# A mixture-of-experts layer on one core: expert rows are added to the residual by the transfers that fetch them

## The reference

```python
h = tok(x)
h = h + attn(layernorm(h))
# ffn, on xf = layernorm(h)
probs = softmax(xf @ router_w)
topw, topi = top_k(probs, 2)
combine = zeros.at[row, topi].add(topw)
ye = einsum('nef,efd->ned', silu(einsum('nd,edf->nef', xf, w1)), w2)
routed = einsum('ne,ned->nd', combine, ye)
shared = silu(gate) * up @ shared_down          # gate, up = xf @ shared_gate_up
shared = sigmoid(xf @ shared_gate_w) * shared
out = h + routed + shared
```

## Time and profile before

| | us |
|---|---|
| median of three runs | 1132.4 |
| lowest and highest | 1131.16, 1133.53 |
| the profiled execution | 1139.81 |
| its span, first to last instruction | 1138.0 |

### The profile page before, as it was taken

The page is one execution under the profiler, slowest core; times in us unless marked ns, Lnnn a source line. Parts: engine busy times, 40 slices in busy tenths (PEclk is TensorE's granted clock), DMA queues, the critical chain, the costliest instruction groups (busy, mean ns, idle before and its releaser), DMA issues.

```text
span 1138.0 us, 24005 instructions
## 1 busy us (share of the span) xinstructions
PE 1062.1 (93%) x8058; PEld 891.3 (78%) x8059; DVE 768.7 (68%) x1975; ACT 671.1 (59%) x2062; POOL 537.2 (47%) x575
## 2 busy tenths in 40 slices
PE   7979999999999999999999999999979798899985
PEld 6857788878877887877788788788858687898874
DVE  3757766785776678577667857766765954566666
ACT  4647765774775677477567747766774333454431
POOL 0025434554556455464545546454361746544542
PEclk9989999999999999999999999999999988999997
DMA  8110000000001000000100000010025423343494
GB/s 259 56 43 2 1 1 19 2 11 30 20 2 38 20 1 13 27 20 2 38 20 1 20 20 20 1 39 20 2 98 194 134 70 108 112 134 121 131 330 141
DMA packets 46624, 66.07 MB, mean 58 GB/s; under 512 B 7992, under 2 KB 39608, under 8 KB 45496
## 3 DMA queue, kind: packets, MB, share of 16 engines
q1 hardware_dynamic: 39720, 46.73, 13.1%
q0 software_dynamic: 6528, 17.97, 4.3%
q10 hardware_dynamic: 272, 0.00, 0.0%
HBM read 36.22 MB, written 28.46 MB: 57 GB/s over the span
## 4 chain that ended last, share of the span: by engine, by line
PE 72%; DVE 8%; issue 6%; POOL 5%; ACT 2%; another core or an unknown queue 1%; DMA 0%; DVEq 0%; SPq 0%; ACTq 0%; POOLq 0%
PE pT_ps L730 10%; PE o_ps L743 9%; PE proj_ps L68 9%; PE proj_ps L70 9%; PE proj_ps L69 9%; PE s_ps L716 8%; PE v_ps L68 2%; POOL prob L1676 2%; PE v_ps L69 2%; PE v_ps L70 2%; PE s_ps L68 2%; POOL prob L1678 2%; PE s_ps L70 2%; PE pT_ps L977 2%; PE s_ps L69 2%
## 5 line engine op out<-in xcount | busy, mean ns | idle before, releaser
L1039 ACT ACTIVATE prob<-s_ps,nmax 128x255 f32<-128x255 f32 x512 | 239.1, 478 | 227.7 <-DVE nmax L1251 227.6
L1676 POOL TENSOR_SCALAR prob<-prob,rinv 128x255 f32<-128x255 f32 x128 | 139.6, 1090 | 373.8 <-DVE rinv L1269 369.4
L1251 DVE TENSOR_REDUCE nmax<-s_ps 128x2 f32<-128x510 f32 x256 | 166.0, 681 | 37.9 <-PE s_ps L716 36.4
L730 PEld LDWEIGHTS pT_ps<-ident,prob 128*128 128x128 f32 x1024 | 109.8, 141 | 60.6 <-issue 49.7
L730 PE MATMUL pT_ps<-ident,prob 128*128 128x128 f32 x1024 | 146.2, 281 | 6.5 <-POOL prob L1678 3.4
L743 PE MATMUL o_ps<-probT,v 128*64 128x256 f32 x1024 | 139.6, 394 | 1.2 <-DVE oT_lo L1282 1.2
L1276 DVE COPY probT<-pT_ps 128x512 f32<-128x512 f32 x128 | 88.4, 691 | 77.0 <-PE pT_ps L730 77.0
L716 PE MATMUL s_ps<-qk_space 64*128 64x256 f32 x1536 | 125.2, 295 | 5.1 <-ACT prob L1039 4.4
L1678 POOL TENSOR_SCALAR prob<-prob,rinv 128x255 f32<-128x255 f32 x128 | 119.1, 931 | 0.0
L716 PEld LDWEIGHTS s_ps<-qk_space 64*128 64x128 f32 x1536 | 98.9, 185 | 21.8 <-issue 8.5
L1771 POOL DMA_INDIRECT expert_out_rows<-yg,y_at x72 | 69.4, 964 | 81.1 <-DVE yg L1581 45.4
(11 more groups left out here) (267 smaller groups left out, 2778.2 us busy)
## 6 DMA issues: line engine op xcount, KB each, us to landing
xg<-expert_in_rows SPq DMA_DIRECT2D x72, 130.0 KB
back<-expert_out_rows SPq DMA_DIRECT2D x8, 1024.0 KB, 9.4
xin<-in_x_dram SPq DMA_DIRECT2D x8, 512.0 KB, 4.4
z_rows<-z SPq DMA_DIRECT2D x8, 512.0 KB, 3.2
z<-z_rows SPq DMA_DIRECT2D x8, 512.0 KB
expert_in_rows<-bo_row SPq DMA_DIRECT2D x16, 128.0 KB
raw_up<-in_L_ffn_w_dram SPq DMA_DIRECT2D x8, 256.0 KB, 5.0
raw_down<-in_L_ffn_w_dram SPq DMA_DIRECT2D x8, 256.0 KB, 6.3
```

The lines of the kernel that those rows point to most:

```text
L730: m = pe.transpose(pT_ps[h][:, o:o + P], prob[u_par(i)][:, h, qt, kt * P:(kt + 1) * P], ident[:])
L1039: m = act.activation(prob[u_par(i)][:, h, qt, 1:N], s_ps[h][:, qt * N + 1:(qt + 1) * N], ACT.Exp, bias=nmax[u_par(i)][:, n:n + 1], accum_o ...
L1251: dve.tensor_reduce(nmax[u_par(i)][:, 2 * h:2 * h + 2], s_ps[h][:].rearrange("p (q k) -> p q k", q=2)[:, :, 1:N], AX_X, ALU.max, negate=Tr ...
L1676: pool.tensor_scalar(prob[k][:, 0, 1, 1:N], prob[k][:, 0, 1, 1:N], rinv[k][:, 1:2], None, ALU.mult).then_inc(s_nA1, 1)
```

## The change

The two results of a token no longer stand side by side: choice 0 of token r goes to row r of `y_rows`, choice 1 to row 4096 + r. The tiles `back`, the loads into them, and all additions of expert rows on DVE and POOL are gone. In their place POOL issues, for each group and choice, one transfer from `y_rows` in HBM to the group's rows of `resid` in SBUF with `accum_op=ADD`: 16 transfers of 512 KB. For a group the second choice's transfer waits until the first one's has landed. For groups 0 to 3 the first one waits for the gated addition, which was done before the loop. For groups 4 to 7 the order is turned round: the gated addition (`add_shared`) waits until both transfers have landed. A store waits for both. The issue order on POOL is 4, 5 (first), then 4, 5 (second) and 0, 1 (first), then 0, 1 (second), then 2, 3, 6, 7 (first) and 2, 3, 6, 7 (second), with `hidden_split_lo` of groups 4 and 5 in between and that of 6 and 7 behind them all.

```diff
             def store_group(g):
-                sp.wait_ge(s_all, g + 1)
+                sp.wait_ge(s_back[g], 16 * TOP)
                 sp.wait_ge(s_added, 2 * g + 2)
...
             load_z3(SHARED_EARLY + 2)
-            for k in range(UNROLL):
-                sp.wait_ge(s_yst[k], 16 * TURNS)
-            for g in range(2):
-                load_back(g)
             load_z3(SHARED_EARLY + 3)
-            for g in range(2, 5):
-                load_back(g)
             for g in range(GROUPS):
                 store_group(g)
-                if g + 5 < GROUPS:
-                    load_back(g + 5)
...
             def add_shared(g):
                 dve.wait_ge(s_gate, 2 * g + 2)
-                if g >= EXPERTS_FIRST:
-                    dve.wait_ge(s_all, g + 1)
-                else:
-                    dve.wait_ge(s_woe, 2 * g + 2 + FREE_W)
+                if g >= SHARED_EARLY:
+                    dve.wait_ge(s_back[g], 16 * TOP)
+                dve.wait_ge(s_woe, 2 * g + 2 + FREE_W)
...
-            pool.iota(dest_u[:], pattern=[[TOP, GT]], base=0, channel_multiplier=TOP * GT).then_inc(s_iotas, 1)
+            pool.iota(dest_u[:], pattern=[[1, GT]], base=0, channel_multiplier=GT).then_inc(s_iotas, 1)
...
-            pool.tensor_scalar(dest[:], dest_u[:], float(-TOP * GR), None, ALU.add)
+            pool.tensor_scalar(dest[:], dest_u[:], float(-GR), None, ALU.add)
...
-                        pool.tensor_scalar(z2_twice[:, n, :, D], dest[:], float(n), None, ALU.add)
+                        pool.tensor_scalar(z2_twice[:, n, :, D], dest[:], float(n * ROWS), None, ALU.add)
...
+            def add_experts(g, k):
+                if k:
+                    pool.wait_ge(s_back[g], 16)
+                else:
+                    pool.wait_ge(s_woe, 2 * g + 2 + FREE_W)
+                    if g < SHARED_EARLY:
+                        pool.wait_ge(s_added, 2 * g + 2)
+                rows = y_rows[ROWS * k + GR * g:ROWS * k + GR * (g + 1), :].rearrange("(p t) d -> p (t d)", t=GT)
+                pool.dma_start(resid[:, GT * g:GT * g + GT, :].rearrange("p t d -> p (t d)"), rows,
+                               accum_op=ALU.add).then_inc(s_back[g], 16)
+
+            for k in range(UNROLL):
+                pool.wait_ge(s_yst[k], 16 * TURNS)
+            for g in (4, 5):
+                add_experts(g, 0)
             hidden_split_lo(4)
-            pair_rows(0)
+            for g in (4, 5):
+                add_experts(g, 1)
+            for g in (0, 1):
+                add_experts(g, 0)
             hidden_split_lo(5)
-            pair_rows(2)
+            for g in (0, 1):
+                add_experts(g, 1)
+            for g in (2, 3, 6, 7):
+                add_experts(g, 0)
+            for g in (2, 3, 6, 7):
+                add_experts(g, 1)
             hidden_split_lo(6)
-            pair_rows(4)
             hidden_split_lo(7)
```

More of the change, by code:

```diff
@@ L469, in main_phase @@
         raw_up, raw_down = (over(n, first, 0, [DC, E, F]) for n, first in (("raw_up", at["oT_lo"]), ("raw_down", wo_at)))
-        back = [over(f"back{g}", (at["oT_hi"], at["oT_lo"], at["qk_space"], wo_at)[g // 2], g % 2 * GT * TOP * D,
-                     [GT, TOP, D]) for g in range(GROUPS)]
         xgT_hi, xgT_lo = ([over(f"{n}{k}", at["probT1"], (2 * j + k) * DC * P, [DC * P], F32R) for k in range(2)]
@@ L524, in main_phase @@
         s_back = [sem(f"back{g}_in") for g in range(GROUPS)]
-        s_pair, s_first, s_gate = sem("expert_rows_paired"), sem("first_added"), sem("gates_ready")
-        s_all, s_out = sem("rows_complete"), sem("out_stored")
+        s_gate = sem("gates_ready")
+        s_out = sem("out_stored")
         s_pgo = sem("pool_wait_met")
-        PAIRED_BY_POOL = (0, 2, 4)
-        EXPERTS_FIRST = 6
         def uses(r, k):
@@ L1599, in _ @@
             y_copy(TURNS - 1, UNROLL - 1)
[L1601 to L1613, removed]
             z3_lo(4)
@@ L1619, in _ @@
             z3_lo(5)
-            add_experts(0)
             product(5, 0)
@@ L1623, in _ @@
             z3_lo(6)
-            add_experts(1)
-            add_experts(2)
             add_shared(4)
             product(6, 0)
-            add_experts(3)
             product(6, 1)
             z3_lo(7)
-            add_experts(4)
             add_shared(5)
             product(7, 0)
-            add_experts(5)
             product(7, 1)
-            add_experts(6)
-            add_experts(7)
             add_shared(6)
@@ L1688, in router_step @@
                 elif i == 4:
-                    pool.tensor_scalar(dest[:], dest[:], float(TOP * GR), None, ALU.add).then_inc(s_dest, 1)
+                    pool.tensor_scalar(dest[:], dest[:], float(GR), None, ALU.add).then_inc(s_dest, 1)
                     pool.wait_ge(s_dest, r + 1)
@@ L1782, in _ @@
                     scatter(r, k)
-            def pair_rows(g):
-                pool.wait_ge(s_back[g], 16)
-                pool.tensor_tensor(back[g][:, :, 0, :], back[g][:, :, 0, :], back[g][:, :, 1, :], ALU.add).then_inc(s_pair, 1)
+            def add_experts(g, k):
[12 more added lines that the diff above has]
+                add_experts(g, 0)
             hidden_split_lo(4)
-            pair_rows(0)
+            for g in (4, 5):
+                add_experts(g, 1)
+            for g in (0, 1):
+                add_experts(g, 0)
             hidden_split_lo(5)
-            pair_rows(2)
+            for g in (0, 1):
[4 more added lines that the diff above has]
+                add_experts(g, 1)
             hidden_split_lo(6)
-            pair_rows(4)
             hidden_split_lo(7)
```

## The result

| | before | after |
|---|---|---|
| median, us | 1133.53 (5 runs) | 1140.54 (5 runs) |
| lowest and highest | 1131.16, 1134.7 | 1139.23, 1142.33 |
| the profiled execution | 1139.81 | 1139.23 |
| its span | 1138.0 | 1137.5 |

The changed kernel is slower: ratio 1.0066, 95% interval 1.0049 to 1.0083, 7.0 us between the medians. I had forecast 1136.5 us, a span 4.2 us longer than before's; the time lies inside the range.

A forecast was written before the change was run, and what follows sets the result against it. Before, DVE was late; after, DMA work of 41.6 + 13.2 + 2.5 = 57 us would fill a 55 us stage. Steps to 1138.5 plus 3.7 us gave span 1142.2, 4.2 us longer; on median 1132.4, 1136.5 us, range 1121 to 1164.

The forecast's parts named there:

- What bounds the kernel, DVE: Last stage before: DVE is late, with 21.8 us of expert-row additions; PE waits 7.3 us for a gated addition.
- The DMA engines of before: Last stage before: engines full from 1085 to 1095 with eight 1 MB loads, which bound only the stage's start.
- Two passes, 2.6 us: Each accumulating 512 KB transfer takes two plain passes of the DMA engines, 2.6 us, 41.6 us for 16; chance 0.45.
- B: Rival: an accumulating transfer costs one pass, 16 take 20 us, PE is the bound, time 1117 to 1120; chance 0.12.
- B': Rival: an accumulating transfer costs between one and two passes, 1.3 to 2.3 us, giving 1120 to 1134; chance 0.18.
- C: Rival: an accumulating transfer costs three passes in turn, 3.8 us, span 1161 and time 1155; chance 0.25.
- slope of 1.6 us per 0.1 us: Each 0.1 us on the size of an accumulating transfer was to move the span by 1.6 us.
- Start of the transfers: First halves of groups 4 and 5 issue at 1082.6, start 1.0 us later and end at 1088.8, in unmoved times.
- The middle: From the landing of group 0's first half to group 6's gated addition: 31.0 us, including three groups' stores, 4.95 us.
- Shared rows of group 6: After its stand, PE runs these 24 matmuls at clock 0.50 in 5.5 us, ending at 1130.4 in unmoved times.
- legs of PE and DMA: Two paths to the last gated addition's end: PE's through group 7's shared rows, 1138.1; the transfers' landing, 1138.5 (unmoved).
- The tail, 3.7 us: Stores between the end of the last gated addition and the end of the span, 3.7 us as before.

The follow-up runs named there:

- e10: Order of e9, but VectorE adds all eight groups' expert rows, with no GpSimd pair sums and no adding transfer; ratio 0.9948 to before.
- e9: Kernel before in the new layout, groups 6 and 7 by adding transfer, VectorE's other additions behind the products, no GpSimd pair sums; ratio 0.9892 to before.
- e8: Changed kernel with all stores held back until every accumulating transfer had landed; a single run, last stage 68.4 us.
- e1: Changed kernel with its 16 transfers as plain copies that overwrite instead of adding, same order and waits; ratio 0.9916 to before.
- e3: Kernel before with the new row layout alone, all additions still on DVE and POOL; ratio 0.9993 to before.
- e4: Kernel before in the new row layout, with accumulating transfers for groups 6 and 7 alone; ratio 0.9983 to before.

## Why the prediction was right, step by step

Times of the prediction are moved by 6.8 us here, since the stage began that much earlier.

- **What bounds the kernel, DVE.** Right in kind: DVE's gated additions came late. But what made them late was their place more than their sum. e10 leaves DVE nearly as much to add (20.9 us, 16 instructions) in another order and without POOL's sums, and its stage is 52.5 us; four additions less give 49.1 (e9). I also took the 1843 and 1413 ns of the earlier trace rows for what an addition costs; alone it is 1.23 us, 16.0 us for the 13 instead of the 21.8. The rest is overlap with POOL in the trace of before: 3.9 us in four additions beside low parts (2.17 to 2.22 us each), which stay in every kernel, and 2.0 us beside one pair sum.
- **The DMA engines of before.** I had its loads bound only the start. The trace has shares of 1.00, 0.95, 0.93 and 0.88 in the four windows from 1095 to 1115 as well, with loads and stores: less room than I read.
- **Two passes, 2.6 us.** Right in kind: full share at half the rate, 1.93 to 1.98 times a plain copy. The Trainium skill (Collectives: The Full Stack, section on the bandwidth ceiling and the fold count) has a ratio of 1.93 between a collective that copies and one that adds; the traces agree. In size 2.49 us (e8) where I had 2.6. B, B' (up to 2.3 us) and C are out. My slope of 1.6 us per 0.1 us was too steep for my own steps: the first two transfers end before POOL can issue the next, so 14 count, 1.4 us. The upper end of B', 1134, is 2 us too high as well: 0.3 us less for 16 transfers gives 1131.7.
- **Start of the transfers.** The first half of group 0 landed at 1095.9 where the steps give 1093.0, 2.9 us later. No data moved before 1078 (the DMA share is 0.00 from 1076 to 1078) where the steps have 1076.8, and 0.8 us of that is POOL's later issue. The last input load, issued at 1081.80, goes in among the first transfers; I had counted its 1.3 us in the total of 57 us and not in the steps. Where the remaining 0.4 us went isn't shown.
- **POOL's issue, 1.0 us.** 0.86 us, and 0.53 for a plain copy; hidden, as said.
- **`hidden_split_lo(6)`.** It began at 1117.26 where the steps give about 1115.5. PE stood 12.6 us; the steps give 12.2, and the "some 11" among my signs was a slip.
- **The middle.** Between the landing of group 0's first half and the gated addition of group 6 the steps have 31.0 us, the trace 29.3: 1.7 less. Ten transfers at 2.49 us are 24.9, and 0.9 us of idle DMA time from 1096 to 1099 comes on top, which the steps don't have. By this estimate 3.5 us were left for stores, where the steps had three groups, 4.95 us. What did not go here went into the tail.
- **Shared rows of group 6**: 5.5 us at clock 0.50, as forecast. **Those of group 7**: 2.9 us where I had 5.5, 2.6 us too high. The clock had come back to 2.4 GHz by 1126.25, after 5.5 us of matmuls; in the trace of before the stand lay right ahead of the last block, and this one has a block in between.
- **The last gated additions.** Those of group 6 started at 1125.2 (steps: about 1124.0), the last of group 7 ended at 1130.24 (steps: 1131.7). My legs of PE and DMA met within 0.4 us; in the trace PE's came last, 0.29 us of wait.
- **The tail, 3.7 us: the term that was mis-sized.** It took 7.26 us. I carried it over from before, where one store was left at that point. My own steps placed only five of eight stores ahead of the last transfer; three were left, 5 us by my 1.65 us a group, and each is 1.8 us alone. The trace after has six groups issued from 1119.35 on, and 1.97 MB (263 GB/s for 7.5 us), nearly four groups, still to move behind 1130.

The sum of the steps was 63.1 us for the stage and 65.3 was measured: +3.5 for the tail, +2.9 for the start, -1.7 for the middle and -2.6 for the clock leave +2.1 of the +2.2. Of the 4.0 us by which the median lies above my 1136.5, these are about half; another 1.1 us is that before itself measured 1133.53 in the comparison, where I had started from 1132.4; the rest is not placed. So the mechanism was right, and the closeness of the number was in part luck: 6.4 us too low in two terms against 4.3 too high in two others.

## What to carry to other kernels

An accumulating transfer is not a free addition: it takes an addition off an engine and asks nearly twice the DMA time of the copy. Add up the DMA engines' work over the whole stretch, stores included, before giving it all of a stage's additions; give it only as many as fit (here four or six of 16, together with an order in which the other additions fill gaps). Look for the order first: in this kernel it gave, without POOL's sums, about half of the gain (0.9948 against 0.9892) without any new transfer. And a second engine that helps with additions on SBUF may cost the first one more than it takes off it: compare the mean of an instruction beside the helper with its mean alone.

## What the runs showed of the hardware

- A 512 KB transfer from HBM that adds to SBUF took 2.49 us of all 16 DMA engines (210 GB/s, e8), a plain one on the same queue 1.29 us (407 GB/s, e1). Its issue on GpSimd took 0.86 us against 0.53.
- A VectorE addition of 128x1024 floats with both inputs in SBUF took 1.21 to 1.23 us alone, 1.7 to 2.2 beside one GpSimd subtraction, and 3.02 and 6.76 beside GpSimd's sums of 128x1024: longer by about the time that the two overlapped (1.8 us for 1.9, 5.5 for 5.4, 1.0 for 1.1).
- Stores of output rows moved at 289 GB/s with the DMA share at 0.94 (e8), well below the loads' 416.
- Profiled executions on one chip, with the same row layout and expert loop, differ in the granted clock at the start of that loop (from 905 to 930, 0.73 in e3 and 0.87 in e4), and the last stage starts 5.5 us apart (1079.70 and 1074.17). So the spans of two profiles mislead where a change is worth less than that.
